# Thirty-two block products of each of the last two FFN inputs: from one VectorE instruction to one ScalarE instruction per block

## What is computed

```python
def fake_quant_nvfp4(x, global_scale):
    xb = x.reshape(sh[:-1] + (sh[-1] // BLOCK, BLOCK))          # BLOCK = 16
    amax = jnp.max(jnp.abs(xb), axis=-1, keepdims=True)
    sc = jnp.clip(amax / FP4_MAX * global_scale, 0.0, FP8_MAX)
    sc8 = sc.astype(jnp.float8_e4m3fn).astype(jnp.float32)
    dq = sc8 / global_scale
    safe_dq = jnp.where(dq == 0.0, 1.0, dq)
    a = jnp.clip(jnp.abs(xb) / safe_dq, 0.0, FP4_MAX)
    q = jnp.sign(xb) * _FP4_VALS[jnp.digitize(a, _FP4_MIDS)]
    return (q * dq).reshape(sh)

hidden = silu(nvfp4_linear(x, gate_w)) * nvfp4_linear(x, up_w)
out = nvfp4_linear(hidden, down_w)
```

## Time and profile before

| | |
|---|---|
| median of 3 runs | 567.04 us (565.94 to 567.5) |
| profiled execution | 565.97 us, its span 564.2 us |
| mean granted clock of TensorE | 0.991 |
| busy: PE, DVE, ACT, POOL | 523.3, 499.7, 335.6, 336.4 us |

### The profile page before, as it was taken

How to read it: one execution, slowest core, us unless ns; L and a number is a source line. 1 busy time by engine, 2 the same in 40 slices (tenths; PEclk the granted TensorE clock), 3 DMA queues, 4 the chain that set the end, 5 groups by cost and what they waited for, 6 DMA issues and landing times. The chain is left out here.

```text
span 564.2 us, 14568 instructions
## 1 busy us (share of the span) xinstructions
PE 523.3 (93%) x6022; PEld 374.5 (66%) x6031; DVE 499.7 (89%) x678; ACT 335.6 (59%) x559; POOL 336.4 (60%) x258
## 2 busy tenths in 40 slices
PE   7899999999899999999999999999999877878876
PEld 7777767777567777777776777777777543444433
DVE  5788888899889888889899999899889999989997
ACT  3755655655555665468475765676568464856644
POOL 3121324323327776767888879977898894745660
PEclk9999999999999999999999999999999998989998
DMA  8910000000110011101110111011100000000001
GB/s 216 319 68 2 3 1 3 3 2 1 42 40 1 12 40 48 46 4 50 49 30 21 49 48 34 18 48 48 35 17 9 9 2 17 0 21 19 20 19 57
DMA packets 16644, 20.77 MB, mean 37 GB/s; under 512 B 2821, under 2 KB 14322, under 8 KB 16578
## 3 DMA queue, kind: packets, MB, share of 16 engines
q1 hardware_dynamic: 14800, 19.18, 11.4%
q10 hardware_dynamic: 1778, 0.66, 0.6%
HBM read 16.16 MB, written 1.84 MB: 32 GB/s over the span
## 5 line engine op out<-in xcount | busy, mean ns | idle before, releaser
L435 POOL TENSOR_TENSOR work<-work,rden 125x1792 f32<-125x1792 f32 x48 | 172.5, 3593 | 3.8
L1045 ACT ACTIVATE work<-scores 125x896 f32<-125x896 f32 x96 | 88.9, 987 | 89.1 <-PE scores L1548 89.1
L715 DVE TENSOR_REDUCE negmax<-scores 125x112 bf16<-125x1792 f32 x48 | 97.1, 2023 | 17.9 <-PE scores L1538 17.2
L723 DVE TENSOR_REDUCE den<-work 125x56 f32<-125x896 f32 x96 | 102.5, 1067 | 7.7 <-ACT work L1045 7.5
L433 POOL TENSOR_TENSOR rden<-rden,stays 125x112 f32<-125x112 f32 x48 | 21.9, 457 | 62.9 <-DVE rden L728 62.8
L1538 PE MATMUL scores<-qz,kT 32*125 32x224 f32 x768 | 49.8, 373 | 3.6 <-ACT work L1045 2.9
L1574 PE MATMUL head_out<-work,v 125*32 125x112 f32 x1536 | 48.7, 265 | 0.3 <-POOL work L435 0.3
L1645 PE MATMUL wide<-ctxT,ck 128*128 128x375 f32 x128 | 48.6, 500 | 0.0
L1548 PE MATMUL scores<-negmax,identb 125*125 125x448 bf16 x192 | 45.4, 359 | 2.5 <-DVE negmax L715 2.2
L1659 PE MATMUL wide<-cv,ctxT 128*125 128x256 f32 x192 | 46.7, 379 | 0.0
L728 DVE RECIPROCAL rden<-den 125x112 f32<-125x112 f32 x48 | 40.9, 852 | 1.4
(11 more groups left out here) (283 smaller groups left out, 1132.3 us busy)
## 6 DMA issues: line engine op xcount, KB each, us to landing
ctx_sb<-in_ctx SPq DMA_DIRECT2D x16, 375.0 KB
mask_sb<-in_mask_Bx1xSxS_if SPq DMA_DIRECT2D x16, 164.1 KB, 5.5
xsx<-in_x SPq DMA_DIRECT2D x4, 448.0 KB, 10.0
out_x<-ores SPq DMA_DIRECT2D x6, 256.0 KB, 2.4
a_raw_w<-in_L_ffn_gate_w SPq DMA_DIRECT2D x1, 1024.0 KB, 8.7
a_raw_w<-in_L_ffn_up_w SPq DMA_DIRECT2D x1, 1024.0 KB, 11.2
a_raw_w<-in_L_ffn_down_w SPq DMA_DIRECT2D x1, 1024.0 KB, 13.3
xt<-xsx SPq DMA_DIRECT2D x4, 112.0 KB, 2.2
```

The costliest lines, as they stand in the source:

```text
L435: pool.tensor_tensor(ex2[0:KP, kc], ex2[0:KP, kc], over, ALU.mult).then_inc(s["prob"], 1)
L715: dve.tensor_reduce(negmax[0:KP, :], scores[0:KP, :, 0:4 * TOK].rearrange("p j (h t) -> p t j h", h=4), AX.XY, ALU.max, negate=True).then_ ...
L723: link(dve.tensor_reduce(den[0:KP, kc, half], ex2[0:KP, kc, :, half, :].rearrange("p g t s -> p t g s"), AX.XY, ALU.add))
L1045: act.activation(ex2[0:KP, kc, 4 * i:4 * i + 4].rearrange("p (j m) t s -> p j m s t", m=NE), scores[0:KP, 2 * i:2 * i + 2, 0:4 * TOK].rear ...
```

## The change

The product of pairs 5 and 6 goes from VectorE's list to ScalarE's. On VectorE it was one tensor_tensor over 128 x 512, with each inverse spread over its block. On ScalarE it is one Identity activation for each block, 128 x 16, with that block's column of `inv` as the scale per partition: 32 for each pair, 64 in all. They stand at k=1 and k=3, right ahead of `x_magnitude`. The two waits move along with them, and the last of each 32 raises `x_t`.

```diff
@@ VectorE
-                def x_units_here(p):
-                    dve.wait_ge(s["inv"], 2 * (p - (NPT - 2)) + 1)
-                    dve.wait_ge(s["x_r"], p)
-                    dve.tensor_tensor(blocks(x_t[:]), blocks(x_unit[:]), spread(inv[:, HBK:HBK + XBK], XBK), ALU.mult
-                                      ).then_inc(s["x_t"], 1)
...
-                    if k in (1, 3):
-                        x_units_here(NPT - 2 + k // 2)
                     if k < NPT:
                         rounded(k - 1)
@@ ScalarE
+                def x_units_here(p):
+
+                    act.wait_ge(s["inv"], 2 * (p - (NPT - 2)) + 1)
+                    act.wait_ge(s["x_r"], p)
+                    for n in range(XBK):
+                        last = act.activation(x_t[:, n * BLK:(n + 1) * BLK], x_unit[:, n * BLK:(n + 1) * BLK], ACT.Identity,
+                                              scale=inv[:, HBK + n:HBK + n + 1])
+                    last.then_inc(s["x_t"], 1)
...
                     if k in (1, 3):
+                        x_units_here(NPT - 2 + k // 2)
                         x_magnitude(NPT - 2 + k // 2)
```

## The result

The changed kernel takes 578.07 us (median of 4 runs, 577.5 to 578.49) against 566.92 us for the kernel before (565.94 to 567.5): 1.0204 times as long, with a 95% interval of 1.019 to 1.0218, or 11.2 us more. The forecast was 579.1 us, 575.5 to 585.0, slower. The profiled executions took 578.13 and 565.97 us, spans 576.4 and 564.2; they differ by 12.2 us, since the one of before lies 1 us under its median.

The account below looks back on a forecast made before the run. In the FFN loop VectorE, almost never idle, was taken as the bound. Waits 11.9 us, TensorE's clock +0.6 and a non-recurring stretch -0.4 gave 12.1 us more: 578.1 us profiled, 579.1 us median, range 575.5 to 585.0.

Parts of the forecast that it names:

- The two waits: VectorE's x_mag step waits for ScalarE's 32 activations, one every 0.207 us: +5.64 us at k=1, +6.24 at k=3.
- The removed product worth nothing in the changed kernel: VectorE, k=1 and k=3: dropping the tensor_tensor (0.87 and 0.60 us) only makes VectorE wait longer for x_mag.
- Nothing gives the wait back: FFN loop behind each wait: VectorE's own row of work decides again, so nothing recovers the 11.9 us delay.
- The rounded copies hidden behind the block maximum: ScalarE behind x_magnitude: copies over by about 484.3, wanted about 486, cost nothing; without that cover about 1 us each time.
- TensorE's clock behind the waits: TensorE at k=2 and k=4 idles, then runs at half clock: 0.3 us each, +0.6 together, range 0 to 2.5.
- The stretch at k=3 that need not come again: TensorE's half clock at 499 to 503 delayed the xT copy 0.9 us; it may not recur: -0.4 us taken.
- The sum: Whole kernel: 11.9 + 0.6 - 0.4 = 12.1 us, so 578.1 us profiled and 579.1 us as a median.
- no overlap: Rival, ScalarE: small activations do not overlap, one every 0.299 us; 5.7 us more, 584.8 us; chance 0.07.
- shorter pitch: Rival, ScalarE: activations start every 0.16 us, as from PSUM; 2.9 us less, 576.2 us; chance 0.05.
- only sixteen: Rival, ScalarE: only sixteen activations a pair, as the title says; 6.6 us less, 572.2 us; chance 0.02.
- The clock stays low long: Rival, TensorE: clock stays low long behind both waits; 1.9 us more, 581.0 us; chance 0.06.
- Hidden: Rival, ScalarE before x_magnitude: activations overlap so deeply x_mag is in time; 1.2 us less, 565.8 us; chance 0.02.

Follow-up runs that it names:

- one-block: Changed kernel with only the first of 32 blocks multiplied on ScalarE at k=1 and k=3, the other products left out: 566.35 us, ratio 0.9994 to before.
- half: Changed kernel with sixteen activations of 128x32 instead of 32 of 128x16 at each place, same columns: 571.56 us, ratio 1.0097 to before.
- double kernels: Changed kernel with each of the 32 activations done twice, first into a spare tile: 591.84 us, ratio 1.0449 to before.
- the moved wait: Changed kernel with VectorE's x_mag step placed behind the next iteration's scales, ScalarE's list unchanged: 575.05 us, ratio 1.0151 to before.
- the filled one: Changed kernel with idle matmuls on TensorE (15 at k=2, 22 at k=4) ahead of gate(k,0): 578.53 us, ratio 1.0208 to before.
- the GpSimd one: Kernel before with both pairs' product as one tensor_tensor on GpSimd behind units(k-1): 567.23 us, ratio 1.0011.
- the kernel with the earlier product: Kernel before with the product still on VectorE but ahead of hidden(k,1) at k=1 and k=3: 566.75 us, ratio 1.0001.

## Why the prediction was right, point by point

- **The two waits**: right in mechanism, place and size. 5.37 and 5.98 us were measured, 5.64 and 6.24 forecast. The difference, 0.53 us, is the pitch: 0.199 us rather than 0.207 (62 x 0.008 = 0.5). The row of two x_sh gave one rounded difference between two starts. The Trainium skill (ScalarE: Activation LUTs, What ACT_TABLE_LOAD costs) gives 0.199 by its figures, and the trace agrees with it within a nanosecond, better than with my reading of the row. VectorE's idle time at k=3 was 5.93 us and not 6.8. Of the difference 0.26 us is the pitch, 0.33 the string's start (3.07 us behind hidden(3,1), before 3.40), and 0.32 VectorE's own steps from hidden(3,1) to the wait (4.36 us, against 4.64 less the 0.60 of the product before). The one-block, half and double kernels show that this cost is the count times the pitch and nothing else.
- **The removed product worth nothing in the changed kernel**: right. VectorE's L854 ends at 477.0 and then it waits until 482.9.
- **Nothing gives the wait back**: right. Twice the string cost 12.8 us more in the profiled executions (13.8 by the medians), 12.7 by its length.
- **The rounded copies hidden behind the block maximum**: right. They end at 483.78, and VectorE asks for them at 485.78 without idle time. The 1 us for the case that this cover were gone is tested by no run: in the moved wait the block maximum still stood ahead of them, and the 4.2 us there are the wait for the whole string, met from an earlier point of VectorE's list.
- **TensorE's clock behind the waits**: right that it falls, too small. In the profiled execution it took 0.33 us at k=2 (forecast 0.3) and 1.02 at k=4, of which 0.37 was given back in the next iteration, so 0.65 (forecast 0.3). TensorE idled 4.33 and 6.09 us, forecast 5 to 6. At k=2 it took up work at full clock, at 485.59, and the granted clock was 0.75 in 486 to 487 and 0.50 to 489; at k=4 it had fallen within the wait, to 0.61 in 517 to 518, and stayed at 0.50 until 524, so some 4.8 us of work ran at half clock and not 3.4. With k=3 alone on ScalarE the way from the x_mag step to hidden(4,1) is 8.54 us, only 0.32 over the kernel before: the size of this term changes with where the stretch falls.
- **The stretch at k=3 that need not come again**: it did not come in the profiled run, and the string began 1.0 us less late than hidden(2,1) had been (forecast 0.4). From one x_mag step to the other it is 33.6 us rather than the 34.6 forecast, 0.7 of it by this stretch and 0.3 by the pitch. Other kernels here have it again (the filled one and the GpSimd one), so that it stayed away is not a merit of the change.
- **Not foreseen**: 0.36 us at k=5, where VectorE started 0.46 us after ScalarE's magnitude ended rather than 0.10, and 0.6 us behind hidden(6,1), where TensorE ran at half clock from 562 to 568 (before: from about 551 to 554.4). The first has no cause that the runs show, and that the second comes from the clock is read from the rows and not tested.
- **The sum**: 578.1 in the terms of the profiled execution, 578.13 measured. That is closer than the parts deserve, since the waits were forecast 0.5 too long and the rest 0.6 too short; that they cancel is luck. For the median it was 579.1 forecast and 578.07 measured, 12.1 us more against 11.2: the profiled execution of before lies 0.95 us under its median, that of the kernel after at its own.
- **The rivals**: "no overlap" (0.299) and "shorter pitch" (0.16) are refuted by the row itself, "only sixteen" by the count of 64 (the loop's own count, 32 a pair, is also what this document's title says). "The clock stays low long" (581.0) came in part: some 6.8 us at k=4, 3.4 at k=2. Its price was too high: 1.36 us behind both waits, where 2.5 had been put down. "Hidden" was priced at 1.2 us for VectorE's freed time; the one-block kernel shows 0.75 in the trace and no difference that its runs can tell. The step that failed there: I took VectorE's row of work as its own clock. Without the product L849 runs beside GpSimd at k=3 too (0.28 us), and L852 waits for ScalarE's magnitude, and that for GpSimd (0.15 for both).

## What to carry to other kernels

A loop over blocks with a scale for each partition pays a whole instruction for each block: here 0.199 us for 16 columns, of which 0.013 us is columns. One instruction with a spread operand on a busier engine (0.6 to 0.9 us) beats 32 on an idle one, since what counts is how long the next engine in line waits and not whose busy share is lower. Before moving work, compare the length of the string with the gap between the ready time and the wanted time at that very place (1.2 and 0.6 us here). And look at which third engine the freed engine waits for anyway.

## What the runs showed of the hardware that was not expected

- VectorE and GpSimd delay each other, in both directions and in instructions that had looked harmless: GpSimd's 128x512 product 1.06 to 2.04 us behind VectorE's L856, VectorE's bf16 tensor_scalar 0.43 to 1.09, L855 1.21 to 1.75 in the kernel with the earlier product, and there GpSimd's pair of 128x1024 products 3.83 to 4.27 beside VectorE's x_t product, which itself took 1.21 rather than 0.68. Where the end of the first of two can be read, the second ends as if it had begun 0.13 to 0.15 us before it: L849 of the changed kernel at 475.31 less 1.21 is 474.10, and GpSimd's pair ended at 474.23.
- A stretch of TensorE at half clock is not tied to one place. Behind the two waits 1.36 us were gained by filling them, 1.0 was lost at k=3 and 0.6 at the end, and the medians show no gain. The four runs of the filled kernel took 576.77, 578.02, 579.04 and 579.44 us at a mean granted clock of 0.994, 0.991, 0.988 and 0.988.
- 64 small activations of ScalarE kept the same pitch from the first to the last (6.46 us for the first 32, 6.44 for the second), where none of the rows read before showed more than four in a row.
